# A second norm's aggregation moved behind the bank scaling, a combination's low half moved ahead of the residual, on VectorE

## What is computed

```python
h = layernorm(x) * (1 + ca) + sa                     # first norm, modulated
q = h @ Wq.T                                         # 16 heads of 32
sigma = elu(q) + 1
a = einsum(sigma, memories) / clip(einsum(sigma, memory_norms), 1e-6)   # 4 banks a head
combined = einsum(a * active, softmax(bank_weights)) # the banks weighted and summed
x = x + ga * (combined @ Wo.T)                       # gating and residual
h = layernorm(x) * (1 + cb) + sb                     # second norm, modulated
x = x + gb * (sparsify_2to4(silu(h @ w_gate) * (h @ w_up)) @ w_down)
```

## Time and profile before

| | before |
|---|---|
| median of 3 runs | 1441.78 us (1441.34 to 1442.45) |
| the profiled execution | 1442.22 us |
| its span, first to last instruction | 1440.4 us |
| TensorE busy | 1394.2 us, 97% |
| VectorE busy | 881.5 us, 61% |
| ScalarE busy | 507.4 us, 35% |
| GpSimd busy | 547.2 us, 38% |
| mean granted TensorE clock | 0.993 |

### The profile page before, as it was taken

How to read it: one execution, slowest core, us unless ns; L and a number is a source line. 1 busy time by engine, 2 the same in 40 slices (tenths; PEclk the granted TensorE clock), 3 DMA queues, 4 the chain that set the end, 5 groups by cost and what they waited for, 6 DMA issues and landing times.

```text
span 1440.4 us, 18863 instructions
## 1 busy us (share of the span) xinstructions
PE 1394.2 (97%) x6866; PEld 1139.9 (79%) x6866; DVE 881.5 (61%) x1260; ACT 507.4 (35%) x793; POOL 547.2 (38%) x367
## 2 busy tenths in 40 slices
PE   8999999998989999999999999999999999999997
PEld 4588888887768888888888887778888888888885
DVE  6777777778575636555555657574645555463654
ACT  5466666665622222122122233332222212222211
POOL 1755665666053313131332334462313223231311
PEclk9999999999999999999999999999999999999999
DMA  6302112213420202021010302230201101020102
GB/s 242 117 31 117 66 80 87 87 58 125 168 89 7 96 0 95 11 84 61 33 66 29 124 29 95 88 124 1 95 25 69 66 29 69 26 95 0 66 0 95
DMA packets 23657, 102.41 MB, mean 71 GB/s; under 512 B 2629, under 2 KB 3141, under 8 KB 13901
## 3 DMA queue, kind: packets, MB, share of 16 engines
q1 hardware_dynamic: 23628, 102.05, 18.9%
HBM read 68.47 MB, written 33.57 MB: 71 GB/s over the span
## 4 chain that ended last, share of the span: by engine, by line
PE 78%; DVE 12%; issue 4%; ACT 3%; DMA 1%; POOL 1%; DVEq 0%; SPq 0%; ACTq 0%
PE bank L1111 25%; PE bank L1113 24%; PE bank L1112 24%; DVE banks_r L936 2%; PE bank L1132 1%; PE bank L1182 1%; DVE h_abs L1063 1%; PE bank L1120 1%; DVE one_each L1051 1%; DMA wmod_sb<-in_wmod_dram 1%; DVE x_ring L899 1%; DVE combT_lo L905 1%; PE bank L1192 1%; DVE pair_lo L1045 1%; DVE ln_raw L767 1%
## 5 line engine op out<-in xcount | busy, mean ns | idle before, releaser
L1026 DVE TENSOR_TENSOR h_act<-bank,silu_g 128x512 f32<-128x512 f32 x128 | 88.1, 690 | 408.8 <-PE bank L1113 388.1
L451 POOL TENSOR_TENSOR hs_lo<-h_abs,hs_hi 128x512 fp32r<-128x512 f32 x128 | 174.7, 1395 | 417.6 <-ACT hs_hi L671 417.6
L403 POOL TENSOR_TENSOR h_lo<-h_raw,h_hi 128x512 fp32r<-128x512 f32 x64 | 125.1, 1983 | 238.8 <-ACT h_hi L654 238.8
L1111 PE MATMUL bank<-h_hi,up_w_hi 128*128 128x512 f32 x512 | 200.7, 392 | 7.7 <-DVE h_act L1026 6.0
L1111 PE MATMUL bank<-h_hi,gate_w_hi 128*128 128x512 f32 x512 | 200.6, 392 | 7.3 <-ACT silu_g L677 4.5
L1111 PE MATMUL bank<-down_w_hi,hs_hi 128*128 128x512 f32 x512 | 200.1, 391 | 2.4 <-POOL hs_lo L451 2.4
L1112 PE MATMUL bank<-h_lo,up_w_hi 128*128 128x512 f32 x512 | 200.0, 391 | 0.0
L1113 PE MATMUL bank<-h_hi,up_w_lo 128*128 128x512 f32 x512 | 199.9, 390 | 0.0
L1112 PE MATMUL bank<-h_lo,gate_w_hi 128*128 128x512 f32 x512 | 199.9, 390 | 0.0
L1112 PE MATMUL bank<-down_w_lo,hs_hi 128*128 128x512 f32 x512 | 199.9, 390 | 0.0
L1113 PE MATMUL bank<-h_hi,gate_w_lo 128*128 128x512 f32 x512 | 199.9, 390 | 0.0
(11 more groups left out here) (133 smaller groups left out, 2393.2 us busy)
## 6 DMA issues: line engine op xcount, KB each, us to landing
h_raw<-h2T_scratch SPq DMA_DIRECT2D x16, 1024.0 KB, 4.8
x_ring<-in_x_dram SPq DMA_DIRECT2D x8, 1024.0 KB, 4.9
x_scratch<-x_ring SPq DMA_DIRECT2D x8, 1024.0 KB, 3.9
h2T_scratch<-h_full SPq DMA_DIRECT2D x8, 1024.0 KB, 3.9
over_x<-x_scratch SPq DMA_DIRECT2D x8, 1024.0 KB, 4.9
acc_scratch<-over_x SPq DMA_DIRECT2D x8, 1024.0 KB, 3.9
over_x<-acc_scratch SPq DMA_DIRECT2D x8, 1024.0 KB, 4.8
out_dram<-over_x SPq DMA_DIRECT2D x8, 1024.0 KB, 3.9
```

The source lines that it names most:

```text
L403: nc.gpsimd.tensor_tensor(h2_lo[:, k], h2_raw[:, k], h2_hi[:, k].bitcast(F32), ALU.subtract).then_inc(h2_lo_done, 1)
L451: nc.gpsimd.tensor_tensor(hs_lo[:, j], h_abs[:, j], hs_hi[:, j].bitcast(F32), ALU.subtract).then_inc(hs_lo_done, 1)
L1026: nc.vector.tensor_tensor(h_act[:, cc, j], bank[2 * (j % 2) + 1][:], silu_g[:, j % 2], ALU.mult).then_inc(h_done, 1)
L1111: nc.tensor.matmul(out_, stat[0], mov[0], start=start, stop=False)
```

## The change

In VectorE's tile, for tiles 1 to 7, two things move. The low half of subtile 0's transposed combination goes from behind `attn_rest` of the tile before's last subtile to between its gating and its residual. And the four scalings of subtile 2's banks go ahead of the aggregation and `ln_var` of the second norm; the wait for the statistics (`bn2_done`) stands ahead of the scalings now. Tile 0 keeps its order. Nothing is added or left out, and the other engines' programs are the same.

```diff
--- before.py
+++ after.py
@@ -984,18 +984,19 @@
                     next_scalars()
                 scale_banks(u + 1, 1, first)
                 invert_norms(u + 2, 0, first)
-                if not first:
-                    attn_rest(t - 1, 3, u - 1)
-                    dve.wait_ge(bn2_done, 4 * t)
-                combT_low(u, 0)
+                if first:
+                    combT_low(u, 0)
+                else:
+                    attn_rest(t - 1, 3, u - 1, between=lambda: combT_low(u, 0))
                 if last:
                     split_w_low(SPLITS[0])
 
+                if not first:
+                    dve.wait_ge(bn2_done, 4 * t)
+                scale_banks(u + 2, 0, first)
                 if not first:
                     ln_aggregate(t - 1, 1, ag2_done)
                     ln_variance(1)
-                scale_banks(u + 2, 0, first)
-                if not first:
                     ln_scalars(t - 1, 1)
                 if first:
                     dve.wait_ge(ga_in, 16 * B)
```

## The result

The changed kernel is slower: 1464.11 us median of four runs (1462.03 to 1464.52) against 1442.12 of the kernel before (now also four runs, 1441.34 to 1445.0), ratio 1.015, 95% interval 1.0134 to 1.0165. The forecast was 1463. Its profiled execution took 1463.79 us around a span of 1462.0, so 21.6 us more than the span of before, 1440.4. The mean granted TensorE clock is 0.985 instead of 0.993.

A forecast was written before the change was run, and what follows sets the result against it. TensorE, busy 97%, was taken to bound the kernel, its first-phase transposes held by ScalarE's root. Delay 13.8, last tile 1.6 and clock falls 6.0 sum to 21.4 us on 1441.78: 1463 us, range 1455 to 1469.

The forecast's parts named there:

- What bounds: First phase: TensorE, busy 97%, waits for h1_full, queued on ScalarE behind the root that waits for ln_var; slack about 0.2 us.
- Part 1: Low half ahead of the residual: TensorE's first half product starts 0.94 us sooner, of 1.04 waited; swallowed by the root's delay.
- Part 2: Four scalings ahead of the aggregation: root, h1_full and TensorE 2.30 us later in each of tiles 1 to 6, 13.8 us.
- Part 4: TensorE's clock falls behind the new 3.2 us gap: 1.2 us in five of six tiles, 6 us.
- Part 3: Last tile: root 2.19 us later, product 1.1 later; tile costs 1.6 us, between 1.1 and 2.2, clock counted as nothing.
- The sum: Whole kernel: 13.8 + 1.6 + 6.0 = 21.4 us added to the median 1441.78, giving 1463 us.
- Rival A: Tiles 1 to 6: the new gap is bridged at full clock, 13.8 + 1.6, 1457 us; chance 20%.
- Rival B: Nothing TensorE needs hangs on the later root, so only 7 x 0.94 = 6.6 us gained, 1435 us; chance 4%.

The follow-up runs named there:

- e5: Changed kernel with ScalarE's root behind h1_full 3 in tiles 1 to 6, scale and shift moved between next gating and low half; 1434.62 us, ratio 0.9934.
- e1: Changed kernel with aggregation and ln_var back ahead of the scalings, low half still between gating and residual; 1442.33 us, ratio 0.9995 to the kernel before.
- e2: Changed kernel with the low half back behind the residual's statistics, aggregation and ln_var still behind four scalings; 1462.15 us, ratio 1.0128 to the kernel before.
- e4: Changed kernel with aggregation and ln_var behind two of the four scalings; 1451.01 us, ratio 1.0048 to the kernel before.
- e10: Changed kernel with aggregation and ln_var behind three of the four scalings; 1455.45 us, ratio 1.0091 to the kernel before.
- e3: Changed kernel with 12 extra TensorE matmuls a tile ahead of the transposes waiting for h1_full, tiles 1 to 6; 1458.05 us, ratio 1.0089 to the kernel before.

## Why the prediction was right, and where it was off

**What bounds.** That ScalarE's root carries `h1_full` with it, and TensorE's transposes behind that, is shown by e5: moving the root behind it, with the scale and shift that need the root, turned 1.015 into 0.9934.

**Part 1**, 0.94 gained at the first wait and all of it swallowed: right. The product started 0.04 from the forecast time, and in e1 the gain didn't show. The Trainium skill ("VectorE: DVE Perf Modes", The DRAIN you can't avoid) measured eight tensor copies with a semaphore behind each as long as with one behind the last. The 128x512 steps here behave otherwise: VectorE's starts were 0.58 to 0.60 apart where a step doesn't wait for the one in front and 0.71 where it does (228.65, 229.23, 229.83, 230.54), and e2's low half shows it once more, 0.61 against 0.73. The root came 2.34 later (234.37 - 220.46 - 11.57), between the 2.30 worked out from the rows and the 2.40 by that page, since the scalings started 0.82 behind the statistics and not 0.73.

**Part 2**, 2.30 a tile: 42.17 - 39.86 = 2.31, measured. e4 and e10 show its slope, 0.60 for each scaling, and e3 that it is a pure delay.

**Part 4**, the clock: forecast 1.2 us in five of six tiles, 6 us; measured 1.5 in four of six, 6 us. The kind was right (most gaps, not all); that the sum was right with both factors off in opposite ways is luck. e3 shows that it is TensorE's idleness in the gap that does it. The Trainium skill ("TensorE: Matmul & The Clock Gate", Part 1) says that the point of the change differs from run to run; here gaps of one length ended differently within one run: tiles 1 and 4 kept the clock, the other four not. That is not all chance, since e2 kept it in tiles 1 and 4 too (periods of 42.10) and lost it in 2, 3 and 5.

**Part 3**, the last tile, was forecast at 1.6 and came to 2.6 in the profile after (4.09 less 1.5 for tile 6's fall). The order's share was right. The product started at 371.60, 22.66 behind the 348.94 of before, and 21.55 of that are from ahead (20.05 between the L508 of tile 6, 320.50 and 300.45, and 1.5): +1.1. What was off is the clock's share, "I count it as nothing either way". During the whole product the clock was down, and it had fallen before the wait of 3.28 began:

```profile
365.70 0.39 PE L1183 MATMUL bank<-mem_hi,sigma_hi 64*128 64x256 f32 x2 [1.36 <-DVE banks_r L936]
...
371.60 0.77 PE L1112 MATMUL bank<-wo_hi,combT_hi 128*128 128x512 f32 x1 [3.28 <-DVE x_ring L899]
```

```profile
core 0: us, PE busy (x) PEld busy (x) DVE busy (x) ACT busy (x) POOL busy (x), PEclk, DMA share, GB/s
367.00:368.00 1.00, 1.00 (x12) 1.00 (x12) 0.66 (x6) 0.64 (x3) 0.00 (x0) 0.59 1.05 410
368.00:371.60 3.60, 0.32 (x5) 0.06 (x3) 1.99 (x4) 3.60 (x8) 3.44 (x3) 0.50 0.25 96
371.00:377.00 6.00, 5.40 (x13) 4.17 (x14) 4.31 (x8) 5.86 (x4) 5.92 (x6) 0.50 0.43 141
```

The wait of 1.36 for VectorE's scalings, which stand behind the weight split here, is one that the forecast didn't have. From 371.60 to the next transposes at 376.86 the product took 5.26 us, where the kernel before took 2.83 (348.94 to 351.77). Part of that went into the 0.56 us that TensorE had waited for the combination before; the transposes of the combination came 24.63 later (378.01 against 353.38), which is 3.08 net of the 21.55, where the forecast had 2.19.

e3_filled has the same last tile, and there the clock stayed up over the wait and fell only behind it, for two thirds of the product:

```profile
363.43 0.56 PE L1112 MATMUL bank<-wo_hi,combT_hi 128*128 128x512 f32 x1 [3.73 <-DVE x_ring L899]
```

```profile
core 0: us, PE busy (x) PEld busy (x) DVE busy (x) ACT busy (x) POOL busy (x), PEclk, DMA share, GB/s
359.70:363.40 3.70, 0.00 (x0) 0.01 (x1) 2.09 (x5) 3.70 (x8) 3.41 (x3) 1.00 0.28 108
363.40:367.10 3.70, 3.67 (x9) 2.96 (x10) 3.57 (x7) 3.70 (x3) 3.70 (x4) 0.54 0.17 50
```

There the product took 4.41 us, the transposes of the combination came 2.08 later than before, counted from L508 of tile 6, and the tile cost 1.53 (92.93 against 91.40), near the forecast's 2.19 and 1.6. So the last tile is about 1.6 where the low stretch is as short as it was before the change, and 2.6 in the execution that was profiled after it. One trace of each doesn't tell how often it is the one or the other.

**The sum** came out within 1.1 us of the measured median, but partly by luck: tile 0 and the second phase, which the change doesn't touch, contributed +1.5 and -2.5 in the profiled runs, together -1.0, about what the last tile had been forecast short. Rival A (clock holds, 1457) did not come; e3 is that case, made on purpose, at 1458. Rival B, faster at 1435, needed that nothing hang on the root; e5 made it so, and 1434.6 is what it gave, but by a gain of 1.27 in each of six tiles and not the 0.94 in each of seven that it was priced at. (The 2.18 us ahead of tile 7's product, for which the prediction names, stand in the earlier trace rows.)

## To carry to other kernels

Before moving a small step behind larger ones on one engine, look at which engine takes its result next, and what stands behind that taker in its own row: here a root of 0.2 us on ScalarE held back 3 us of work that had nothing to do with it. Of two waits that follow each other closely (for the low half, then for `h1_full`) removing one may only lengthen the other; try the two moves together before calling either useless. And a gap on TensorE is to be priced twice, once for its length and once for the clock behind it: here 2.3 us for the one, and 1.5 in four of six cases for the other.

## What was not expected of the hardware

The same work in the second phase took 1017.97 us between the first and last `pair_hi` in the profile before, 1015.95 after, 1015.56 in e5 and 1018.68 in e1. Most of it is one place, from the 17th to the 18th `pair_hi`: 31.36 before and 31.41 in e1, 29.81 after and 29.77 in e5. The clock tells them apart, the kernel before first, then the changed one, each over the same work (23.65 us later in the second):

```profile
core 0: us, PE busy (x) PEld busy (x) DVE busy (x) ACT busy (x) POOL busy (x), PEclk, DMA share, GB/s
938.00:941.00 3.00, 3.00 (x8) 2.33 (x8) 2.94 (x5) 2.64 (x3) 2.19 (x3) 0.51 0.00 0
961.00:974.00 13.00, 12.56 (x55) 10.42 (x56) 7.77 (x12) 6.01 (x9) 7.50 (x4) 1.00 0.26 67
```

In the kernel before the clock was down there and in the changed one it wasn't. So a single low stretch, in a part that no edit touches, makes two executions differ by 1.5 us. The kernel before ranged from 1440.5 to 1445.5 us, and its mean granted clock goes with it: at 0.993 or 0.994 its executions took 1440.53 to 1442.94 us, at 0.989 or less 1443.47 to 1445.50. What decides whether a gap brings a fall stays open: gaps of 2.0 brought none in six tiles of e4, one of 2.18 was followed by one in the last tile of the kernel before, gaps of 2.6 and 3.2 by three and four in six tiles, and in the last tile of the changed kernel the clock was already down when the gap of 3.28 began.

Twelve matmuls a tile added on the engine that bounds the kernel made it 6 us faster than without them.
